# Pairing the head products of the second attention on TensorE

## The reference

```python
x = x + attn_a(layernorm(x))   # 16 heads of 16, 2048 keys per batch; the values are weighed by the sum of the softmax over the keys
x = x + ffn(layernorm(x))      # relu(x @ W_fc.T)**2 @ W_proj.T, then the mean spikes of a five-step neuron
x = x + attn_b(layernorm(x))   # below
x = x + ffn(layernorm(x))      # the same weights

def attn_b(x):                 # 16 blocks of 256 x 16 columns out of each of two batches
    q, k, v = ((x @ W + b).reshape(b, h, dh, t) for W, b in ...)
    attn = softmax(einsum('bhdt,bhds->bhts', k, v) * temperature)
    return einsum('bhdt,bhts->bhds', q, attn).reshape(b, t, d)
```

## Time and profile before

| | before |
|---|---|
| median of three runs | 2758.28 us |
| span of the profiled execution, first to last instruction | 2751.0 us |
| outside the span, by the median (no separate time is given for the profiled execution) | 7.3 us |
| PE busy | 2361.1 us (86%) |
| DVE busy | 2511.8 us (91%) |
| ACT busy | 2549.7 us (93%) |
| POOL busy | 1282.7 us (47%) |
| largest group on PE | L812, scores of the first attention, 615.3 us |
| products, L731 | 545.7 us busy, 4096 records, 606 ns each |
| mean granted clock of TensorE | 0.981 of full speed |

### The profile page before, as it was taken

The page is one execution under the profiler, slowest core; times in us unless marked ns, Lnnn a source line. Parts: engine busy times, 40 slices in busy tenths (PEclk is TensorE's granted clock), DMA queues, the critical chain, the costliest instruction groups (busy, mean ns, idle before and its releaser), DMA issues. The chain is left out here.

```text
span 2751.0 us, 38753 instructions
## 1 busy us (share of the span) xinstructions
PE 2361.1 (86%) x12438; PEld 1033.2 (38%) x12672; DVE 2511.8 (91%) x2596; ACT 2549.7 (93%) x4763; POOL 1282.7 (47%) x1897
## 2 busy tenths in 40 slices
PE   5788888877787778778778999999999999999997
PEld 2244444443343344344332333333333333333334
DVE  5899999999999999999988999999999999999994
ACT  4899999999999999999988999999999999999994
POOL 0146666655455455555542344434434444443445
PEclk8899999999999999999999999999999999999999
DMA  7521212233311111111111111111111111111110
GB/s 212 121 64 52 69 52 70 60 89 81 73 29 35 43 35 36 36 43 29 43 37 50 38 42 43 38 36 45 42 31 47 43 32 42 43 38 37 44 28 16
DMA packets 190929, 140.77 MB, mean 51 GB/s; under 512 B 92163, under 2 KB 177669, under 8 KB 190726
## 3 DMA queue, kind: packets, MB, share of 16 engines
q1 hardware_dynamic: 190534, 137.76, 18.8%
q10 hardware_dynamic: 192, 0.52, 0.1%
HBM read 92.04 MB, written 41.94 MB: 49 GB/s over the span
## 5 line engine op out<-in xcount | busy, mean ns | idle before, releaser
L1040 DVE TENSOR_REDUCE nmax<-score 128x1 f32<-128x1024 f32 x1024 | 1196.4, 1213 | 101.4 <-PE score L812 95.5
L1013 DVE TENSOR_REDUCE nmax<-score 128x1 f32<-128x1024 f32 x1024 | 1211.0, 1219 | 75.7 <-PE score L750 66.1
L1239 ACT ACTIVATE big<-score,nmax 128x1024 f32<-128x1024 f32 x1024 | 1138.3, 1120 | 69.2 <-DVE nmax L1013 58.2
L1282 ACT ACTIVATE score<-score,nmax 128x1024 f32<-128x1024 f32 x1024 | 1119.4, 1099 | 45.0 <-DVE nmax L1040 43.8
L812 PE MATMUL score<-big,shared 128*128 128x512 bf16 x1956 | 615.3, 395 | 273.9 <-ACT score L1282 236.6
L750 PE MATMUL score<-shared 128*128 128x512 bf16 x1906 | 574.3, 384 | 65.1 <-ACT big L1239 32.7
L731 PE MATMUL bank_g<-big,qw 128*32 128x512 f32 x4096 | 545.7, 606 | 1.0 <-ACT qcol L1267 1.0
L750 PEld LDWEIGHTS score<-shared 128*128 128x128 bf16 x2048 | 138.1, 97 | 594.3 <-ACT big L1239 536.4
L812 PEld LDWEIGHTS score<-big,shared 128*128 128x128 bf16 x2048 | 130.0, 98 | 566.0 <-ACT score L1282 474.0
L706 PEld LDWEIGHTS bank_f<-norms,w_fc_sb 128*128 128x128 f32 x2048 | 278.8, 192 | 75.7 <-ACT hid L1204 37.0
L706 PE MATMUL bank_f<-norms,w_fc_sb 128*128 128x128 f32 x2048 | 297.4, 279 | 10.7 <-ACT hid L1204 9.7
(11 more groups left out here) (145 smaller groups left out, 1653.8 us busy)
## 6 DMA issues: line engine op xcount, KB each, us to landing
shared<-q_parts SPq DMA_DIRECT2D x256, 64.0 KB, 2.5
shared<-kb_parts SPq DMA_DIRECT2D x256, 64.0 KB, 2.3
shared<-vb_parts SPq DMA_DIRECT2D x256, 64.0 KB, 2.3
big<-k_parts SPq DMA_DIRECT2D x48, 192.0 KB, 5.2
big<-k_parts SPq DMA_DIRECT2D x24, 256.0 KB, 7.8
kb_parts<-pieces SPq DMA_DIRECT2D x96, 64.0 KB, 1.6
vb_parts<-pieces SPq DMA_DIRECT2D x96, 64.0 KB, 1.6
shared<-in_x SPq DMA_DIRECT2D x32, 128.0 KB, 2.5
```

The lines of the kernel that those rows point to most:

```text
L1013: v.tensor_reduce(nmax[:, par, c // NCH, c % NCH:c % NCH + 1], score_b(turn, c)[:, :], AX.X, ALU.max, negate=True).then_inc(max_b, 1)
L1040: v.tensor_reduce(nmax[:, par, c // NCH, c % NCH:c % NCH + 1], score_a(turn, c)[:, :], AX.X, ALU.max, negate=True).then_inc(max_a, 1)
L1239: a.activation(expo[:, c // NCH, (c % NCH) * CH:(c % NCH + 1) * CH], score_b(turn, c)[:, :], ACT.Exp, bias=nmax[:, par, c // NCH, c % NCH: ...
L1282: a.activation(s[:, :], s[:, :], ACT.Exp, bias=nmax[:, par, c // NCH, c % NCH:c % NCH + 1], accum_out=esum[:, par, c // NCH, c % NCH:c % N ...
```

## The change

The table of the product's slots is changed, and the code in `phase_b` that reads it. Before, the eight products of a half stand singly, in two neighbouring slots out of three. After, two stand behind each other in one slot out of three: products 0 and 1 of half 1 in slot 7, 2 and 3 in slot 10, 4 and 5 in slot 13, 6 and 7 in slot 16, and those of half 0 in slots 22, 25, 28 and 31. No product stands in slot 0, 6, 9, 12, 15, 23, 26 or 29 any more. In slot 0 the code that placed the entry of 32 goes. The up, down and transpose steps stay where they were. No instruction and no wait is added or removed, on any engine, and the copy of the product on ScalarE stays behind slot 17.

```diff
-PROD_AT = [6, 7, 9, 10, 12, 13, 15, 16], [22, 23, 25, 26, 28, 29, 31, 32]
+PROD_AT = [7, 7, 10, 10, 13, 13, 16, 16], [22, 22, 25, 25, 28, 28, 31, 31]
@@ phase_b of TensorE
-                    if i1 is not None and c + CPT in PROD_AT[1] and not (isinstance(i1, int) and i1 == 0):
-                        product(i1, 0, PROD_AT[1].index(c + CPT))
-                    if i1 is not None and c in PROD_AT[0]:
-                        product(i1, 1, PROD_AT[0].index(c))
+                    for n, at_c in enumerate(PROD_AT[0]):
+                        if i1 is not None and c == at_c:
+                            product(i1, 1, n)
                     if i is not None:
                         head_product(i, c)
```

## The result

The changed kernel takes 2800.84 us, the median of four runs (2797.05 to 2806.63), against 2758.02 before. The ratio is 1.0156 with a 95% interval of 1.014 to 1.0171: slower by 43 us. The prediction was 2805, with 2780 to 2828 as its range. The one before was a short one: wherever a run's time and its span are both given they differ by 1.8 us, so the execution with the span of 2751.0 took about 2753, some 5 us less than the median. The 7.3 us "outside the span" ahead of the prediction are these two together, and the spans, 53.8 us apart, overstate the change by about 11 us.

The account below looks back on a forecast made before the run. No engine alone bounds the second attention, but a ring of TensorE, VectorE and ScalarE. Span 2751, plus 47 (45 for 28 turns, 3 opening, less 1 end), plus 7.3 outside the span, gives 2805 us, range 2780 to 2828.

Parts of the forecast that it names:

- The 7.3 us "outside the span": Whole kernel: the median of 2758.28 exceeds the profiled span of 2751.0 by 7.3 us, taken to stay unchanged.
- The ring: Second attention: score, maximum, exponential, then the score three slots on; pairs delay the next score by 2.38 instead of 1.53.
- the same steps: Second attention: each start worked out slot by slot through a turn as the later of its two or three bounds.
- The sum: Second attention: 1.6 us lost a turn, 45 over 28 turns, plus 3 opening, less 1 end: +47 us.
- the raw end: Second attention: the next turn's first maximum worked out at 41.86 us, 1.4 over the measured turn.
- The opening and the end: Second attention: the four looser opening turns add 3 us; the last, scoreless turn saves about 0.86.
- The number of waits: Second attention: maxima wait for scores eight times a turn, near 0.9 us in each half's first pair, 0.3 to 0.7 otherwise.
- the upper bound: Second attention: every pair's full lateness of 1.01 less six existing waits of 0.31, 6.2 us a turn, +174.
- The cover of the exponential of slot 16: Slot 16: the pair ends near 21.4, the exponential is due at 22.0, so 0.6 us are left.
- TensorE as the bound: Rival, second attention: TensorE sets the pace, so 1.6 us come off each turn, 2713 us; chance 0.04.
- The clock: Rival, second attention: TensorE's clock falls to its lower level for one pair a turn, 2850 us; chance 0.07.
- The half that is made up: Rival, second attention: slots without products give back half of the 1.6 us lost a turn, 2781 us; chance 0.13.

## Why the prediction was right, step by step

- *The ring.* The score behind a pair starts 2.39 after its own slot's score (predicted 2.38), and the nine starts in the table are met within 0.23. The mechanism is shown by the kernels with one pair, with pairs in either half, and with threes: 0.2, 0.8, 0.9 and 3.6 a turn, against 0.2, 0.8, 0.9 and 3.5 that the same steps gave. Half-width pairs in the same slots cost 0.4 to 0.8 instead of 1.7, so it is the length of the block and not what moved.
- *The sum.* I took 1.6 a turn, the difference of two runs through the same steps, rather than 1.4, the raw end against the measured turn. The trace has 1.68. The raw end was 0.22 early, and on the old order the steps end 0.15 early against the settled turn of 40.40, so to take the difference was the right choice. That it is the small things between ScalarE and the next score that they leave out was not tested. 28 turns of 1.68 are 47.
- *The opening and the end.* From the first maximum of turn 0 to that of turn 4 it is 181.5 us after and 181.0 before: 0.5, not 3. The end gave 0.5 back, not 1. So the sum of +47 is met by the trace (47.0 + 0.5 - 0.5) with three terms that were off by +2, -2.5 and +0.5 and cancel: that part is luck. By the profiled spans the difference is 53.8, of which 3.4 had already passed before the first maximum of turn 0 (1395.0 against 1391.6), where nothing was changed, and some 3 are turns with late sums (5 us after, 2 before). The medians are 43 apart, 4 under 47. The interval of the ratio reaches from 39 to 47 us, and the first maximum of turn 0 stands between 1391.6 and 1399.6 in the eleven profiles, so 4 us are within what runs differ by.
- *The number of waits.* I expected eight waits a turn behind the pairs. There are five. The 145 waits before are five a turn as well, and not the six that the upper bound took off; with five it would have been +183 instead of +174. Behind slots 16, 25 and 31 the small steps and statistics on VectorE cover nearly all of the lateness. The steps had it: m(17) is only 0.12 later there than VectorE's own pace allows, m(26) and the next m(0) not at all. The sentence on what to look for counted the pairs instead of reading the steps off.
- *The cover of the exponential of slot 16.* It held, as predicted, by 0.6 us.
- *TensorE as the bound.* The rival was rightly rated low, but by the wrong row. The 633 waits are of weight loads, and most of their time TensorE was still multiplying: its matmuls stood idle behind exponentials for 11.9 of 1160 us. So before the change TensorE was ahead by little. What refutes the rival is that it now stands idle for 92.9 us of 1200.
- *The clock.* The Trainium skill's rule on kernels that cycle through PSUM tiles and idle in between (page "TensorE: Matmul & The Clock Gate", section "A second HAM failure mode: psum-queue depth-cycling") speaks for the rival that came to 2850. This trace doesn't bear it out for these gaps: over 1200 us with waits of mostly 0.2 to 0.85 us before scores the clock is 1.00. The single fall came behind an idle time of 2.59 us that had another cause. With pairs in the second half alone the clock fell three times, behind idle times of 1.94, 2.45 and 1.99 us; behind one of 2.26 in the profile of the whole change, and behind those of 1.70 with the threes, it did not.
- *The half that is made up.* It was not. From slot 17 to 22 the lag went from 0.82 to 0.89.

## What to carry to other kernels

Where engines hand a few tiles around in a ring, what counts on the engine ahead is not only the sum of its work but the longest block between two hand-overs: here, with three tiles, a half-width product of 0.6 us is hidden, a product of 1.0 us leaves short waits of 0.31, and blocks of 1.9 and 2.7 us cost more than the overlap inside them saves. Write down the latency of each link from the trace, close the ring over two periods, and check it against one distance that the trace already shows, before believing a share of busy time. When two orders are compared with a smaller load, look for the wait that stops the faster one, or the distance is misread.

## What was not expected

- Two products directly behind each other overlap by 0.14 us (1.86 against 2 x 1.00 between the starts). The step from a score to a product takes 0.54 (2050.33 to 2050.87) where that to an up step takes 0.44 (2042.91 to 2043.35, same turn), and a pair has it once instead of twice.
- Moving a small step of VectorE, the statistics, by two slots was worth 0.3% of the kernel, and it came to light only where the products had been made cheap.
- Late sums came in three of the 27 turns of the profile of the change, and the clock fell in one of them. The kernel before has four, of 0.2 to 0.4 us, without a fall.
